# Rows of softmax maxima evicted for one head and copied to three by GpSimd, and the values' bias sent once through the output product

## What is computed

```python
x = x + 0.5 * ffn(layernorm(x), gate_w, w1, b1, w2, b2)       # mixture of 8 experts, top 2
x = x + attn(layernorm(x), Wq, bq, Wkv, bkv, Wo, bo)          # causal, 16 heads of 16
x = x + 0.5 * ffn(layernorm(x), gate_w, w1, b1, w2, b2)

def attn(x, Wq, bq, Wkv, bkv, Wo, bo):
    q = x @ Wq.T + bq
    k, v = split(x @ Wkv.T + bkv)
    dots = einsum('bhid,bhjd->bhij', q * scale, k)             # MASK_VAL above the diagonal
    out = einsum('bhij,bhjd->bhid', softmax(dots), v)
    return out @ Wo.T + bo
```

## Time and profile before

| | |
|---|---|
| median of three runs | 1386.14 us |
| the profiled execution's own time | 1391.16 us |
| its span, first to last instruction | 1389.4 us |
| what lies around the span | 1.8 us |
| mean granted TensorE clock | 0.978 of 2.4 GHz |
| PE matmul busy | 1269.6 us (91%) |
| DVE busy | 1095.3 us (79%) |
| ACT busy | 940.9 us (68%) |
| POOL busy | 397.1 us (29%) |

### The profile page before, as it was taken

The page is one execution under the profiler, slowest core; times in us unless marked ns, Lnnn a source line. Parts: engine busy times, 40 slices in busy tenths (PEclk is TensorE's granted clock), DMA queues, the critical chain, the costliest instruction groups (busy, mean ns, idle before and its releaser), DMA issues.

```text
span 1389.4 us, 24415 instructions
## 1 busy us (share of the span) xinstructions
PE 1269.6 (91%) x8356; PEld 549.0 (40%) x8356; DVE 1095.3 (79%) x3527; ACT 940.9 (68%) x1697; POOL 397.1 (29%) x508
## 2 busy tenths in 40 slices
PE   5789999999999999999999999999999999999874
PEld 3223334443344433443344433444334433434332
DVE  5779888878888888878878788887888788779734
ACT  2247776867767777667768677677776677676662
POOL 4223322332223222232322322232222323222111
PEclk9779999999999999999999999999999999999997
DMA  4581443442335443145334424354441344340001
GB/s 140 102 139 30 69 69 58 69 90 63 69 58 99 88 69 69 24 88 99 69 58 69 90 63 71 56 99 88 69 70 26 55 99 69 58 69 31 1 1 33
DMA packets 57827, 95.13 MB, mean 68 GB/s; under 512 B 8352, under 2 KB 51488, under 8 KB 51744
## 3 DMA queue, kind: packets, MB, share of 16 engines
q1 hardware_dynamic: 55664, 92.30, 35.8%
q10 hardware_dynamic: 2032, 1.19, 0.3%
HBM read 59.91 MB, written 33.55 MB: 67 GB/s over the span
## 4 chain that ended last, share of the span: by engine, by line
PE 59%; DVE 19%; ACT 12%; issue 5%; DVEq 2%; POOL 2%; DMA 1%; ACTq 0%; POOLq 0%
PE o_bank L1257 14%; PE s L1238 13%; PE st L1223 11%; PE misc L1176 6%; DVE s L972 5%; ACT q_stack L808 5%; ACT probs L821 5%; DVE max_full L976 4%; PE misc L1148 4%; PE misc L1171 3%; PE misc L504 3%; DVE stats L471 2%; DVE o_tok L1069 2%; POOL probs L695 1%; DVEq L983 1%
## 5 line engine op out<-in xcount | busy, mean ns | idle before, releaser
L821 ACT ACTIVATE probs<-st 128x512 f32<-128x512 f32 (+1 forms) x1216 | 633.2, 583 | 199.6 <-PE st L1223 108.9
L972 DVE CUSTOM_DVE_ANT_0 s<-s,causal 128x128 f32<-128x128 f32 (+3 forms) x1024 | 494.7, 502 | 140.3 <-PE s L1238 137.4
L1238 PE MATMUL s<-k_stack,q_stack 96*128 96x512 bf16 (+3 forms) x1536 | 493.4, 333 | 37.4 <-DVE max_diag L972 14.6
L1223 PE MATMUL st<-q_stack,k_stack 108*128 108x512 bf16 (+3 forms) x1536 | 485.8, 330 | 23.8 <-ACT probs L821 21.5
L976 DVE TENSOR_REDUCE max_full<-s 128x1 f32<-128x512 f32 x512 | 349.9, 683 | 36.6 <-PE s L1238 35.3
L1257 PE MATMUL o_bank<-probs,v_aug 128*17 128x512 f32 (+3 forms) x3072 | 324.3, 494 | 8.7 <-POOL probs L695 6.5
L695 POOL TENSOR_SCALAR_AFFINE_SELECT probs<-probs 128x512 f32<-128x512 f32 x256 | 162.9, 641 | 533.7 <-ACT probs L821 533.5
L1238 PEld LDWEIGHTS s<-k_stack,q_stack 96*128 96x128 bf16 x1536 | 149.3, 98 | 395.8 <-DVE max_diag L972 183.8
L1223 PEld LDWEIGHTS st<-q_stack,k_stack 108*128 108x128 bf16 x1536 | 149.0, 98 | 145.2 <-ACT probs L821 53.8
L707 POOL TENSOR_TENSOR qk<-qk,parts 128x512 f32<-128x512 f32 x64 | 74.6, 1165 | 318.6 <-ACT parts L781 318.6
L972 DVE DVE_READ_ACCUMULATOR2_ANT max_diag<- 128x1 f32 x1024 | 144.6, 141 | 0.0
(11 more groups left out here) (113 smaller groups left out, 867.1 us busy)
## 6 DMA issues: line engine op xcount, KB each, us to landing
part_dram<-parts SPq DMA_DIRECT2D x128, 192.0 KB, 2.8
k_stack<-part_dram SPq DMA_DIRECT2D x186, 128.0 KB, 7.1
q_stack<-part_dram SPq DMA_DIRECT2D x31, 384.0 KB, 5.1
x_all<-x SPq DMA_DIRECT2D x16, 512.0 KB, 11.2
q_stack<-part_dram SPq DMA_DIRECT2D x31, 256.0 KB, 7.5
out<-x_all SPq DMA_DIRECT2D x7, 1024.0 KB, 11.2
q_stack<-part_dram SPq DMA_DIRECT2D x33, 128.0 KB, 9.0
k_stack<-part_dram SPq DMA_DIRECT2D x12, 64.0 KB, 2.9
```

Of the source, the lines that this page charges most:

```text
L821: nc.scalar.activation(probs[:, g % 2, h - part:h + 1, 0:width], st_bank[i % 3][:, 0:share * width] .rearrange("p (h c) -> p h c", c=width ...
L972: nc.vector.tensor_tensor_reduce(out=bank, in0=bank, in1=causal[:, CW - width:CW], scale=1.0, scalar=-BIG, op0=ALU.add, op1=ALU.max, accum ...
L1223: score = nc.tensor.matmul(st_bank[i % 3][:, part * width:(part + 1) * width], k_stack[0:KROWS + MROWS, hg, h, jb * P:(jb + 1) * P], q_sta ...
L1238: nc.tensor.matmul(s_bank[u % 3][:, 0:width], q_stack[0:KROWS, hm, h, ib * P:(ib + 1) * P], k_stack[0:KROWS, hm, h, j0:j0 + width], start= ...
```

## The change

Two things change, and some places in the prologue with them.

1. `mtr`: ACT writes the 12 rows for the first head only (12x512 instead of 12x2048). A new event `mrep`, MREP_LAG = 3 units after `mtr`, lets POOL copy them to the other three heads (12x1536, bf16, SBUF to SBUF), with a drain before and behind it. PE waits for a new semaphore `max_rows_all` ahead of the first `st` of each half.
2. The values' bias: in the prologue a use `bias` multiplies `v_bias`, broadcast over 128 columns, by `w_o` (2 matmuls), ACT evicts 128x256 of it into `xg_t`, and POOL adds it to `bo_row`. `ont` is then evicted by one ACT instruction of 128x512 instead of two of 128x256 with a bias.
3. Prologue: value pairs 2 and 3 move to units 1 and 3 of the `s` walk, and the first projection of step 1, which stood before the walk, moves into it; six projections now stand at units 8 to 53.

```diff
-    "total0": 7, "pro_qk": (8, 19, 30, 41, 52), "pro_before": (5, 12),
+    "total0": 7, "pro_v": (1, 3), "pro_qk": (8, 17, 26, 35, 44, 53), "pro_before": (5, 12),
+MREP_LAG = 3
...
             put(PLACE["mtr"][hg][c], ("use", "mtr", c))
+            put(PLACE["mtr"][hg][c] + MREP_LAG, ("mrep", c))
...
-    plan += [(3, "ones", hq) for hq in range(NG)] + [(3, "use", "v", j) for j in range(4)]
-    plan += [project(1, 0)[0]]
-    jobs = {at: [job] for job, at in zip(project(1, 0)[1:], (3, 5))}
+    if spec:
+        plan += [(3, "use", "bias")]
+    plan += [(3, "ones", hq) for hq in range(NG)] + [(3, "use", "v", j) for j in range(2)]
+    jobs = {u: [(3, "use", "v", j)] for j, u in zip((2, 3), PLACE["pro_v"])}
     for i, u in enumerate(PLACE["pro_qk"]):
-        for job, at in zip(project(1 + (i + 1) // 2, (i + 1) % 2), (u, u + 7, u + 9)):
+        for job, at in zip(project(1 + i // 2, i % 2), (u, u + 7, u + 9)):
...
+            if u == HALF_UNITS[c] + 9:
+                plan.append((3, "mrep", c))
...
+                elif kind == "use" and a[0] == "bias":
+                    eng.wait_ge(sig.misc_free, n("use", 2))
+                    nc.gpsimd.tensor_tensor(bo_row[:, 0, :], bo_row[:, 0, :], xg_t[:, 0, 0:D], ALU.add)
+                elif kind == "mrep":
+                    c, hm = a[0], (hg + 1) % NG
+                    rows, cols = slice(KROWS, KROWS + MROWS), slice(c * CW, (c + 1) * CW)
+                    eng.wait_ge(sig.misc_free, rows_taken[c])
+                    eng.drain()
+                    nc.gpsimd.tensor_copy(q_stack[rows, hm, 1:HG, cols],
+                                          q_stack[rows, hm, 0:1, cols].to_broadcast([MROWS, HG - 1, CW]))\
+                        .then_inc(sig.max_rows_all, 1)
+                    eng.drain()
...
                 elif what == "ont":
-                    for dc in range(DC):
-                        last = nc.scalar.activation(o_t[:, dc, :], bank[:, dc * 2 * P:(dc + 1) * 2 * P],
-                                                    ACT.Identity, bias=v_bias[:, dc:dc + 1])
-                    last.then_inc(sig.misc_free, 1)
+                    nc.scalar.activation(o_t[:, :, :], pair_view(bank), ACT.Copy).then_inc(sig.misc_free, 1)
                 elif what == "mtr":
-                    nc.scalar.activation(q_stack[rows, hm, :, c * CW:(c + 1) * CW],
-                                         bank[rows, :].rearrange("p (o c) -> p o c", o=1)
-                                         .to_broadcast([MROWS, HG, CW]), ACT.Copy)\
+                    nc.scalar.activation(q_stack[rows, hm, 0, c * CW:(c + 1) * CW], bank[rows, :], ACT.Copy)\
                         .then_inc(sig.misc_free, 1)
...
+                elif what == "bias":
+                    for dc in range(DC):
+                        last = nc.tensor.matmul(bank[:, 0:D], v_bias[:, dc:dc + 1].to_broadcast([P, P]), w_o[:, dc, :],
+                                                start=dc == 0, stop=dc == DC - 1)
...
+                    if h == 0 and g in (0, CT):
+                        eng.wait_ge(sig.max_rows_all, lin(b, 2 * NG, 2 * hg + 1 + g // CT))
```

More of the change, by code:

```diff
@@ L285 @@
              "max_done", "mparts_ready", "bo_added", "out_written", "side_full", "side_free",
-             "first_half_in", "late_full", "late_free")
+             "first_half_in", "late_full", "late_free", "max_rows_all")
 Walk = namedtuple("Walk", ("spec", "parts_out", "stack_in") + WALK_SEMS)
@@ L686, in moe_pool @@
                 moe_experts(eng, layer, None, chunk, lambda c, e: eng.nop())
+            rows_taken = {}
             def handle(sig, b, n, hg, kind, *a):
+                if kind == "use" and a[0] == "mtr":
+                    rows_taken[a[1]] = n("use", 2)
                 if kind == "st":
@@ L791, in evict @@
                         .then_inc(sig.misc_free, 1)
+                elif what == "bias":
+                    nc.scalar.activation(xg_t[:, 0, 0:D], bank[:, 0:D], ACT.Copy).then_inc(sig.misc_free, 1)
                 elif what in ("lg", "lg0"):
@@ L844, in handle @@
                     eng.wait_ge(sig.late_full, 1)
-                    for dc in range(DC):
-                        last = nc.scalar.activation(o_t_late[:, dc, :], late_bank[0][:, dc * 2 * P:(dc + 1) * 2 * P],
-                                                    ACT.Identity, bias=v_bias[:, dc:dc + 1])
-                    last.then_inc(sig.late_free, 1)
+                    nc.scalar.activation(o_t_late, pair_view(late_bank[0]), ACT.Copy).then_inc(sig.late_free, 1)
                 elif kind == "weights":
```

## The result

The changed kernel took 1402.9 us in the median of four runs (1399.4 to 1406.4), the kernel before 1388.7 us beside it. The ratio is 1.0092, with a 95% interval of 1.0073 to 1.0112: slower by 0.9%, where 1.9% faster was forecast. (The two medians are 14.2 us apart.) The profiled execution took 1400.20 us, its span 1398.5.

What follows compares the result with a forecast made beforehand. PE was taken as the bound, waiting in places for ACT's eviction of the maxima. Eviction -31, bias -2, copies against DVE +4, prologue +3 gave -26 us: 1360 us against the 1386.14 median, range 1338 to 1379.

Steps and rivals of the forecast that it cites:

- Bounds and prices: PE looks like the bound but waits for ACT's eviction; eviction 0.59 us, `ont` about 0.61, POOL copy 1.6.
- The copy against DVE: POOL's copies in the batches hold some DVE instructions: 0.5 us per batch, 4 us in all, between 0 and 50.
- a sign of being wrong: In the next profile, DVE's L480, L1062 or L989 would show longer means.
- Rival 4: Each copy holds one DVE instruction for half its length, 50 us instead of 4: 1406 us, chance 0.04.
- The eviction: Shorter ACT eviction of the maxima in the batches removes PE and DVE idle time: 31 us, between 16 and 48.
- the part of step 1: Both halves are evicted within 3 us, DVE idles 0.8 us behind them, 8 times: 6.4 us gained.
- the first halves: First-half evictions of steps 0, 2 and 3: PE's idle time, 0.7 us each, goes 23 times, 16 us.
- Group 11's select: Queued behind POOL's copy; in step 2, 2.98 us of room against 1.8 us for copy and drains, zero cost.
- The bias: One `ont` eviction instead of two: 0.5 us in the last chain plus 1.5 elsewhere, 2 us gained.
- The prologue: Six projections in the walk instead of five and moved value pairs cost 3 us, between 0 and 6.
- rival 1: Every eviction sits in the chain, 48 us go instead of 31, copies disturb nothing: 1338 us, chance 0.12.
- rival 2: DVE takes over at once, only the first halves give 16 us, contention and prologue eat 7: 1377 us, chance 0.17.

Runs made afterwards that it cites:

- e2: Changed kernel with POOL's copies also waiting until DVE's normalises listed before them are done: 1373.1 us, ratio 0.9874.
- e8: Kernel before with only the bias change and the single eviction of `ont`, no copies: 1388.0 us, ratio 0.9977.
- e3: Changed kernel with the old wide eviction of all four heads and no copies; bias and new prologue places kept: 1385.7 us, ratio 0.9967.
- e10: e2 with DVE's unmasked maxima taken over 256 of 512 columns, part of the computation left out: 1347.9 us, ratio 0.9683.
- e9: e3 with DVE's unmasked maxima taken over 256 of 512 columns, part of the computation left out: 1365.7 us, ratio 0.9813.
- e4: Changed kernel with the prologue's places as in the kernel before: 1401.3 us, ratio 1.0108.
- e5: Changed kernel with POOL's copy made as three instructions of one head each, in the same place: 1378.6 us, ratio 0.991.

## Why the prediction was wrong

- **Bounds and prices: right.** ACT's eviction did hold PE, and the wait for it fell by 18 us. Eviction, `ont`, copy: 0.59, 0.60, 1.46 us measured; 0.59, 0.61, 1.6 taken.
- **The copy against DVE: this step failed.** I charged 4 us, "0.5 us per batch", because the copies stand away from the splitting of the maxima. I had priced one kind of instruction that POOL holds, L989; the normalise L480 and the cast L1062 I named only as a sign of being wrong, with no price and no look at what stands beside the copies. That sign came: L480's mean went from 450 to 597 ns. DVE's normalises are another kind: one tensor input, SBUF to SBUF, fp32. They stand at units 33 to 36 of step 0 and 13 to 16 of steps 2 and 3, the copies at 36 and 17. The measured cost is 29.8 us (after against e2), 0.48 us per copy where I took 0.06. I also priced a hit as half a copy at random; in step 0 of the second to the seventh batch it is the whole copy every time, and what waits is PE. Rival 4, with the right mechanism, had 0.04. That its 1406 us came so near to 1402.9 is luck: it had 50 us for the copies instead of 29.8, and 31 for the eviction instead of 12.7. Its own argument against itself named only L972, L976 and L989.
- **The rule of the Trainium skill** (GPSIMD Engine Reference, Key points: GpSimd and VectorE share SBUF interfaces, with contention for instructions in a 2-port mode or with two SBUF inputs) was quoted and then weighed too low. The runs agree with it as far as they go: L1005, with two SBUF inputs, takes up to 1.40 us under a copy (0.18 alone), and the normalises and casts from SBUF to SBUF stretch under POOL too, while L988 and L992, whose scores come from PSUM, do not (L992's mean is 683 ns with the copies, and 683 ns in e8, which has none). In which mode an instruction runs no trace here shows.
- **The eviction: mechanism right, size wrong.** The term was 31 us, and 12.7 us came (e3 to e2). Step by step: the part of step 1 came as taken (0.8 us a batch, 0.9 measured), that of step 2 came in part (0.8 taken, 0.5 measured), those of steps 0 and 3 (1.2 each) not at all. For the first halves I took PE's idle time in full, 0.7 us each, and did not ask what PE meets next. It meets the same normalises: in e2 PE waits 0.99 us for them in step 0. DVE's bound held for the first halves too, not only for the second. PE's waits for the masked maxima rose as the wait for Exp fell, first e3, then e2:

```profile
PE s L1257 <- DVE max_diag L987: 8.7, 31, 0.8
```

```profile
PE s L1261 <- DVE max_diag L989: 22.3, 41, 0.8
```

  e10 against e9 shows that a lighter DVE lets more through, but not all.
- **Group 11's select: right**, 1.0 us of slack left.
- **The bias: right.** 2 us taken; e8 measured 3.6 in the medians, with an interval of 1.4 to 4.9, and step 1 of its batches is 0.24 us shorter, 2 us in all.
- **The prologue: +3 us did not come.** e3 against e8 says -2.2, e4 against the changed kernel says that the new places cost 1.6, neither clear of the spread: about zero. The first score tile starts earlier with the new places, by 4.5 us (e8 to e3) and 1.8 us (e4 to the changed kernel); why the end shows less of it stays open. One more projection in the walk did not show as an added DVE gap of 3.3 us: the stretch from 50 to 90 us had a clock of 0.67 before and 0.73 after, and DVE was busy for 31.47 instead of 27.21 us.
- **Two small slips in the sums of the rivals.** With no cost for the copies rival 1 should have kept the prologue's +3, and has +2 (1339, not 1338), and rival 2 leaves out the bias' 2 us (-11, so 1375). Neither changes the forecast.

The steps in the medians are -5.0 us (before to e3: bias and prologue), -12.7 (e3 to e2: short eviction) and +29.8 (e2 to after: the meeting of copy and normalise). That they add up to 1402.9 - 1390.7 is so by construction and confirms none of them. What bears out the last one are the traces. The profiled spans of the changed kernel and e2, 1398.5 and 1371.8 us, are 26.7 us apart: 17.6 are six batches, the second to the seventh, at 2.9 us each, as long as their normalises are held; 6.1 are the four steps in which the granted clock fell (below); the rest lies in the first and the last batch.

## What to carry to other kernels

When work is moved to GpSimd, list every DVE instruction that can run beside it and sort it by where its operands lie: of those that read and write SBUF alone many can be held until the GpSimd instruction ends (here the normalise, the casts and the splitting of the maxima). Not all: L476, the statistics of the layer norm, reads `x_all` in SBUF and writes to SBUF too, and 29 of its 128 began beside a select or another operation of POOL, yet the longest took 0.43 us, like the rest. So look at the longest duration of each line (min/median/max) and not only at its mean. What counts then is who waits for the held instruction, so a single wait that lets the DVE instructions on the path go first can be worth more than the saving itself, and short GpSimd instructions are safer than one long. And PE's idle time behind a stall is a gain only up to the next engine's own lateness: read that engine's list before counting it.

## What was not expected of the hardware

- The hold is exact: a normalise that starts during a POOL copy ends 0.15 us after it, for copies of 0.62, 0.82 and 1.46 us, whether it met the copy 0.01 or 0.33 us after the copy's start, and a second copy right behind does not prolong it (e5). One that starts 0.33 us before a copy takes its usual 0.40 us. What follows the copy's end depends on the held instruction: 0.03 us for the 16 columns of L1005, L1007 and L1009, 0.28 us for the cast of 512 columns, L1078.
- POOL's copy goes by elements: 1462 ns for 1536 bf16, 822 ns for the same bytes as 768 fp32, 618 ns for 512 bf16, though only 12 partitions are used.
- A wait of PE can cost more than itself. In the third batch of the changed kernel PE idles 2.19 us in step 0 and the granted clock stays at 1.00. In the fourth it idles the same 2.19 us, and the clock is 0.87 and then 0.71 in the stretches around it, so at 1.2 GHz for part of them; the eight matmuls of a product take 1.91 us instead of 1.05, and the step 46.1 us instead of 44.6. In four of the batches from the second on a step was longer in this way, three times in step 0 and once, in the sixth batch, in step 3 behind a wait of 1.61 us (granted clock 0.57 from 1024 to 1028 us, the step 40.5 us instead of 38.7). Why the same wait does it in one batch and not in the next no run here shows. The stretches around step 0 of the third batch, then of the fourth:

```profile
424.00:428.00 4.00, 1.81 (x17) 0.82 (x10) 3.72 (x14) 1.96 (x5) 2.23 (x2) 1.00 0.58 137
428.00:432.00 4.00, 4.00 (x35) 1.59 (x33) 3.00 (x13) 2.65 (x5) 0.68 (x2) 1.00 1.12 166
...
588.00:592.00 4.00, 1.81 (x11) 0.92 (x9) 3.38 (x12) 1.60 (x5) 2.16 (x2) 0.87 0.69 161
592.00:596.00 4.00, 4.00 (x29) 1.27 (x28) 1.92 (x9) 1.61 (x5) 0.64 (x1) 0.71 1.01 131
```
